# Pacing a kernel's gathers by TensorE's progress and feeding its pair products from SBUF alone

## The reference

```python
def _L0_rec_ref(inputs, W0, W1):            # inputs (b, 32 fields, 32 dims)
    x = inputs
    res = []
    for W in (W0, W1):
        prev = x.shape[1]
        z = jnp.einsum('bhd,bmd->bhmd', inputs, x).reshape(b, n * prev, k)
        x = jnp.einsum('bpd,pj->bjd', z, W)
        res.append(x)
    return jnp.sum(jnp.concatenate(res, axis=1), axis=-1)
...
e = jnp.stack([tbl_0[ids[:, 0]], ..., tbl_31[ids[:, 31]]], axis=1)
z = _L0_rec_ref(e, L0_rec_W0, L0_rec_W1)
h = jnp.concatenate([z, dense_ctx], axis=1)
h = jnp.maximum(h @ W_top1 + b_top1, 0.0)
h = jnp.maximum(h @ W_top2 + b_top2, 0.0)
y = h @ W_top3
```

## Time and profile before

| | before |
|---|---|
| median of 3 runs | 377.18 us (376.98 to 377.78) |
| span of the profiled execution | 597.7 us |
| own time of the profiled execution | none given beside the span |
| mean granted TensorE clock, profiled | 0.80 |
| PE busy, profiled | 412.6 us |
| DVE busy | 203.4 us |
| ACT busy | 235.5 us |
| POOL busy | 246.5 us |

### The profile page before, as it was taken

How to read it: one execution, slowest core, us unless ns; L and a number is a source line. 1 busy time by engine, 2 the same in 40 slices (tenths; PEclk the granted TensorE clock), 3 DMA queues, 4 the chain that set the end, 5 groups by cost and what they waited for, 6 DMA issues and landing times.

```text
span 597.7 us, 9512 instructions
## 1 busy us (share of the span) xinstructions
PE 412.6 (69%) x3656; PEld 360.8 (60%) x3656; DVE 203.4 (34%) x834; ACT 235.5 (39%) x774; POOL 246.5 (41%) x262
## 2 busy tenths in 40 slices
PE   5512112874257887877788778687787679999988
PEld 4301001653256776766666667577676668989988
DVE  4200000694723333322333233333332235556510
ACT  3300000662175334522343334433452237676641
POOL 6777772547055444544445554544444440000000
PEclk9755555795589877877787888977787779999999
DMA  8100000000000000000000000000000000000000
GB/s 299 45 14 13 13 13 6 11 3 14 2 10 10 8 10 7 10 8 9 9 9 10 10 10 9 11 8 9 8 10 8 8 10 2 2 2 2 2 2 1
DMA packets 10765, 9.66 MB, mean 16 GB/s; under 512 B 4664, under 2 KB 8896, under 8 KB 10720
## 3 DMA queue, kind: packets, MB, share of 16 engines
q0 software_dynamic: 8192, 4.21, 4.8%
q1 hardware_dynamic: 2528, 4.84, 2.3%
HBM read 9.03 MB, written 0.00 MB: 15 GB/s over the span
## 4 chain that ended last, share of the span: by engine, by line
PE 57%; issue 18%; another core or an unknown queue 11%; DVE 7%; ACT 6%; DMA 1%; SPq 0%; ACTq 0%
PE WA L725 20%; PE QB L697 10%; PE PA L687 8%; PE T L710 4%; DVE RT L421 4%; PE M L738 4%; PE M L757 2%; PE ET L674 2%; ACT eblk L285 2%; ACT TS L285 1%; PE PA L639 1%; PE M L764 1%; PE M L748 1%; ACT RT L285 1%
## 5 line engine op out<-in xcount | busy, mean ns | idle before, releaser
L278 POOL DMA_INDIRECT emb<-in_table,rows x256 | 245.8, 960 | 239.0 <-PE ET L674 165.3
L725 PE MATMUL WA<-TS,RX 128*128 128x128 f32 x896 | 127.0, 301 | 1.0 <-ACT TS L285 1.0
L584 DVE COPY TS<-T 32x64 f32<-32x64 f32 x256 | 55.5, 217 | 200.6 <-PE T L710 184.6
L725 PEld LDWEIGHTS WA<-TS,RX 128*128 128x128 f32 x896 | 119.7, 215 | 6.0 <-issue 6.0
L697 PE MATMUL QB<-eblk,zQ 128*64 128x68 f32 x1024 | 69.1, 243 | 74.3 <-issue 74.0
L697 PEld LDWEIGHTS QB<-eblk,zQ 128*64 128x64 f32 x1024 | 49.9, 146 | 89.8 <-issue 85.8
L552 DVE TENSOR_TENSOR zQ<-ET,eT 128x1024 f32<-128x1024 f32 x32 | 39.2, 1225 | 159.0 <-ACT eT L285 158.9
L687 PE MATMUL PA<-eblk,zP 128*128 128x132 f32 x512 | 80.6, 296 | 5.3 <-issue 3.4
L639 PE MATMUL PA<-sym,TS 128*128 128x272 f32 x64 | 29.4, 552 | 74.5 <-issue 47.3
L687 PEld LDWEIGHTS PA<-eblk,zP 128*128 128x128 f32 x512 | 73.4, 212 | 6.3 <-issue 4.9
L285 ACT ACTIVATE eblk<-ET 32x256 f32<-32x256 f32 x128 | 48.6, 380 | 71.0 <-PE ET L674 66.0
(11 more groups left out here) (87 smaller groups left out, 294.1 us busy)
## 6 DMA issues: line engine op xcount, KB each, us to landing
emb<-in_table,rows POOLq DMA_INDIRECT x256
TS<-in_W SPq DMA_DIRECT2D x8, 256.0 KB, 4.3
wt<-in_W_top SPq DMA_DIRECT2D x2, 512.0 KB
y1w<-in_W_rows SPq DMA_DIRECT2D x1, 448.0 KB
TS<-in_W_rows SPq DMA_DIRECT2D x1, 448.0 KB
sym<-in_W_cols SPq DMA_DIRECT2D x1, 264.0 KB, 2.8
TS<-in_W_cols SPq DMA_DIRECT2D x1, 264.0 KB, 3.1
idc<-in_ids SPq DMA_DIRECT2D x1, 128.0 KB, 2.0
```

What stands on the lines that cost most here:

```text
L278: eng.indirect_dma_start(emb[par][:, g, :], None, table, bass.IndirectOffsetOnAxis(rows[:, k, g:g + 1], 0))\
L584: eng.tensor_copy(view(ts[32 * q:32 * q + 32, :, :], P * REST + b0, [[4 * P, 2], [P, 4], [1, 8]]), view(src, q, [[C17, 2], [4, 4], [C33, 8 ...
L725: m = eng.matmul(WA[:, 0:P], C[:, kt, :], TS[k % 2][:, slot_of(kt), :], start=(kt == 0), stop=(kt == KT - 1))
```

## The change

- Gathers 16 to 27 wait for PE's step of W0 x W1 number 2(n - 16) + 9. From gather 28 on, every second gather waits for a step of PE: two gathers for each of the three trios of a unit and two for its last products (`t3_made`), 3.5 units ahead of the unit whose rows they fetch.
- `eT` gets 12 places for each group of eight fields: the eight and the first four again (TURN). ACT fills it with two copies, both ahead of the four into `eblk`, counted by `et_copied`.
- All products read `eT`, none reads ET. The products within a group become cyclic: distances 1 to 3 are one instruction with eight pairs each (768 elements per partition), the four pairs of distance 4 and half of the squares are another (256 elements). The columns' order changes with `off`. NZ goes from 11 to 5.
- The transposes of unit u + 1 stand behind the second trio of unit u (ET_STEP = 1), not ahead of its first. They wait for the copies out of ET only (`et_copied`, `eblk_made`), not for the products. ACT's copies for unit u + 1 move in the same way behind the copy of the second trio. ACT now waits for the products of the unit in front before it writes `eT`, and PE's first trio waits for `eblk_made` as well.

```diff
--- before.py
+++ after.py
@@ -19,6 +19,9 @@
 MORE = 16
 RTC = 2 * P + MORE
 RAB = HALF * HALF
+TURN = SUB + SUB // 2
+FREE = 16
+PACED = 28
 ONES = 16
 SLOTS = 59
 Y1T = 7
@@ -26,7 +29,7 @@
 
 def off(s):
 
-    return sum(SUB - r for r in range(1, s))
+    return SUB * (s - 1) if s <= SUB // 2 else SUB * (SUB - 1 - s) + s
 
 
 def pair_columns():
@@ -73,7 +76,7 @@
     C17 = HALF + 1
     EB = NQ * 2 * C17
     N1, N2 = H1 // P, H2 // P
-    NZ = 11
+    NZ = 5
     W1P = 8
     KT = 56
 
@@ -106,7 +109,7 @@
         wt3 = sb("wt3", [P, N2, P])
 
         emb = [sb(f"emb{i}", [P, P // NQ, D]) for i in range(2)]
-        eT = sb("eT", [P, GROUPS * F])
+        eT = sb("eT", [P, GROUPS * NQ, TURN])
         eblk = [sb(f"eblk{i}", [P, GROUPS, NQ, 2 * C17]) for i in range(2)]
         zP = [sb(f"zP{i}", [P, GROUPS, P]) for i in range(2)]
         zQ = [sb(f"zQ{i}", [P, GROUPS, 2, 64]) for i in range(2)]
@@ -163,6 +166,7 @@
         c_made = sem("c_made")
         c_kept = sem("c_kept")
         et_made = sem("et_made")
+        et_copied = sem("et_copied")
         eblk_made = sem("eblk_made")
         z_made = sem("z_made")
         p_made = sem("p_made")
@@ -236,6 +240,7 @@
 
 
         EARLY_AT = (8, 18)
+        ET_STEP = 1
 
         block = ctx.enter_context(nc.Block())
 
@@ -269,12 +274,24 @@
             eng.wait_ge(const_s, 1)
             eng.affine_select(out=ident[:, :], in_=ident[:, :], compare_op=ALU.not_equal, fill=1.0,
                               base=0, pattern=[[-1, P]], channel_multiplier=1).then_inc(const_s, 1)
+            def gate(n):
+
+                if FREE <= n < PACED:
+                    eng.wait_ge(rt_made, 2 * (n - FREE) + SUB + 1)
+                elif n >= PACED and n % 2 == 0:
+                    u, j = divmod(n - PACED, UG)
+                    if j // 2 < TRIOS:
+                        eng.wait_ge(p_made, TRIOS * u + j // 2 + 1)
+                    else:
+                        eng.wait_ge(t3_made, u + 1)
+
             eng.wait_ge(rows_made, 1)
             for k in range(TILES):
                 par = k % 2
                 for unit in range(UNITS):
                     wait(eng, et_made, UNITS * (k - 2) + unit + 1)
                     for g in range(UG * unit, UG * unit + UG):
+                        gate(UG * UNITS * k + g)
                         eng.indirect_dma_start(emb[par][:, g, :], None, table,
                                                bass.IndirectOffsetOnAxis(rows[:, k, g:g + 1], 0))\
                            .then_inc(gathered[par][unit], 16)
@@ -294,17 +311,19 @@
 
             def eblk_copy(u):
 
+                eng.wait_ge(et_made, u + 1)
+                wait(eng, z_made, NZ * u)
+                parts = ET[:, 0:GROUPS * F].rearrange("p (g i) -> p g i", i=SUB)
+                copy(eT[:, :, 0:SUB], parts).then_inc(et_copied, 1)
+                copy(eT[:, :, SUB:], parts[:, :, 0:TURN - SUB]).then_inc(et_copied, 1)
                 if u == 0:
                     eng.wait_ge(zeroed, 5)
                     eng.wait_ge(ones_set, 4 * NQ)
-                eng.wait_ge(et_made, u + 1)
                 wait(eng, t3_made, u - 1)
                 for v in range(NQ):
                     r = slice(DIM * v, DIM * v + DIM)
                     dst = view(eblk[u % 2][r, :, :, :], 2 * C17 * v + 1, [[EB, GROUPS], [C17, 2], [1, HALF]])
                     copy(dst, ET[r, 0:GROUPS * F].rearrange("p (g x h) -> p g x h", x=2, h=HALF)).then_inc(eblk_made, 1)
-                copy(eT[:, :], ET[:, 0:GROUPS * F]).then_inc(eblk_made, 1)
-
             def part_copy(t):
                 k, j = divmod(t, SLOTS_TILE)
                 unit, r = divmod(j, TRIOS)
@@ -382,9 +401,9 @@
             copy(wt3[:, :, 0], vec[:, N1 + N2:]).then_inc(wt3_made, 1)
             for t in range(TOTAL):
                 u, r = divmod(t, TRIOS)
-                if r == 0 and len(EARLY_AT) <= u + 1 < ALL:
+                part_copy(t)
+                if r == ET_STEP and len(EARLY_AT) <= u + 1 < ALL:
                     eblk_copy(u + 1)
-                part_copy(t)
                 if r == 0 and u > 0:
                     across_copy(u - 1)
                 if r < 2 and u > 0:
@@ -530,41 +549,33 @@
                     apart_across(1, 1, 0, HALF, True, added)
                     cross_second(1, 0, HALF, added)
 
-            def field(a, dims):
-                return view(ET[:, :], a, dims)
-
             def copied(a, dims):
-                return view(eT[:, :], a, dims)
+                return view(eT[:, :, :], a, dims)
 
             def products(u, part):
 
                 parts, sides = 4 * GROUPS, 2 * GROUPS
                 within, across, rest = zP[u % 2][:, :, :], zQ[u % 2][:, :, :, :], z3[u % 2][:, :, :]
 
-                def apart(s):
-                    some = [[SUB, parts], [1, SUB - s]]
-                    eng.tensor_tensor(view(within, off(s), [[32, parts], [1, SUB - s]]), field(0, some), copied(s, some),
-                                      ALU.mult).then_inc(z_made, 1)
-
                 if part == 0:
-                    eng.wait_ge(eblk_made, (NQ + 1) * (u + 1))
+                    eng.wait_ge(et_copied, 2 * (u + 1))
                     wait(eng, t3_made, u - 1)
                     eng.tensor_tensor(view(across, 0, [[64, sides], [SUB, SUB], [1, SUB]]),
-                                      field(0, [[HALF, sides], [1, SUB], [0, SUB]]),
-                                      copied(SUB, [[HALF, sides], [0, SUB], [1, SUB]]), ALU.mult).then_inc(z_made, 1)
+                                      copied(0, [[2 * TURN, sides], [1, SUB], [0, SUB]]),
+                                      copied(TURN, [[2 * TURN, sides], [0, SUB], [1, SUB]]), ALU.mult).then_inc(z_made, 1)
                 if part == 1:
-                    for s in range(1, 5):
-                        apart(s)
+                    turns = SUB // 2 - 1
+                    eng.tensor_tensor(view(within, 0, [[32, parts], [SUB, turns], [1, SUB]]),
+                                      copied(0, [[TURN, parts], [0, turns], [1, SUB]]),
+                                      copied(1, [[TURN, parts], [1, turns], [1, SUB]]), ALU.mult).then_inc(z_made, 1)
                 if part == 2:
-                    for s in range(5, SUB):
-                        apart(s)
-                    some = [[SUB, parts], [1, 4]]
-                    eng.tensor_tensor(view(within, PAIRS, [[32, parts], [1, 4]]), field(0, some), copied(0, some),
-                                      ALU.mult).then_inc(z_made, 1)
-                    some = [[F, GROUPS], [SUB, 4], [1, 4]]
-                    eng.tensor_tensor(view(rest, 0, [[THIRD, GROUPS], [4, 4], [1, 4]]), field(4, some), copied(4, some),
-                                      ALU.mult).then_inc(z_made, 1)
-                    eng.tensor_copy(view(rest, MORE, [[THIRD, GROUPS], [1, HALF]]), field(0, [[F, GROUPS], [1, HALF]]))\
+                    eng.tensor_tensor(view(within, off(4), [[32, parts], [4, 2], [1, 4]]),
+                                      copied(0, [[TURN, parts], [0, 2], [1, 4]]),
+                                      copied(4, [[TURN, parts], [-4, 2], [1, 4]]), ALU.mult).then_inc(z_made, 1)
+                    eng.tensor_tensor(view(rest, 0, [[THIRD, GROUPS], [4, 4], [1, 4]]),
+                                      copied(4, [[NQ * TURN, GROUPS], [TURN, 4], [1, 4]]),
+                                      copied(4, [[NQ * TURN, GROUPS], [TURN, 4], [1, 4]]), ALU.mult).then_inc(z_made, 1)
+                    eng.tensor_copy(view(rest, MORE, [[THIRD, GROUPS], [SUB, 2], [1, SUB]]), copied(0, [[NQ * TURN, GROUPS], [TURN, 2], [1, SUB]]))\
                        .then_inc(z_made, 1)
 
             def rest_copies(u, part):
@@ -668,7 +679,8 @@
             def emb_transposes(u):
                 k, unit = divmod(u, UNITS)
                 eng.wait_ge(gathered[k % 2][unit], 16 * UG * (k // 2 + 1))
-                wait(eng, z_made, NZ * u)
+                wait(eng, et_copied, 2 * u)
+                wait(eng, eblk_made, NQ * u)
                 for q in range(2):
                     g = UG * unit + NQ * q
                     t = eng.transpose(ET[:, P * q:P * q + P], emb[k % 2][:, g:g + NQ, :].rearrange("p g d -> p (g d)"), ident[:, :])
@@ -679,6 +691,7 @@
                 u, r = divmod(t, TRIOS)
                 if r == 0:
                     eng.wait_ge(z_made, NZ * (u + 1))
+                    eng.wait_ge(eblk_made, NQ * (u + 1))
                 if t == 0:
                     eng.wait_ge(rt_kept, F)
                     eng.wait_ge(rx_kept, F // 2)
@@ -799,9 +812,9 @@
                     emb_transposes(EARLY_AT.index(h))
             for t in range(TOTAL):
                 u, r = divmod(t, TRIOS)
-                if r == 0 and len(EARLY_AT) <= u + 1 < ALL:
+                triples(t)
+                if r == ET_STEP and len(EARLY_AT) <= u + 1 < ALL:
                     emb_transposes(u + 1)
-                triples(t)
                 if r == TRIOS - 1:
```

## The result

The changed kernel takes 401.77 us (median of five runs, 397.35 to 402.67) against 377.18 (376.60 to 377.78): a ratio of 1.063 [1.059, 1.067]. The forecast was slower, by 11.5 us; it is slower by 24.6. The time lies in the range of 369 to 412.

The account below looks back on a forecast made before the run. POOL's chain of gathers was taken as the bound, 369.7 us before. After: 338.2 (last gather landed) + 38.0 (remainder) + 4.9 (hold) = 381.1, 11.5 more; 377.18 + 11.5 = 388.7 us, range 369 to 412.

Parts of the forecast that it names:

- Which chain ends last: PE's chain put at 366.2 us, POOL's chain of gathers at 369.7 before the change; POOL's the longer.
- The prediction's own test: If removing the gate alone doesn't win back some 6 us, the gathers' chain is not what sets the end.
- the gate's term: Gather 60 waits for tile 1's first trio and starts at 88.7 us instead of 79.2; POOL never catches up.
- the hold's term: Gathers meeting SBUF-only products on DVE take longer: 0.2 us per unit, 4.9 us over 24.5 units.
- last gather to the end: Behind unit 31's transposes, now 2.9 us later in unit 30, 38.0 us remain instead of 40.95.
- around the span: The 7.5 us from POOL's chain of 369.7 us to the median of 377.18, taken as lying around the span.
- the landing: A gather takes 5.8 us from start to landed, read from the first unit's last gather.
- long lock: Rival: runs of SBUF-pair work on DVE hold gathers long; 413 us at 1.2 us per unit, 445 at 2.5; chance 0.16.
- The transposes' place: Behind the second trio, 4.4 us from transposes to products is hidden under 5.4 us of PE work; costed at nothing.
- The products: Eleven DVE instructions become five, the cyclic ones 0.95 and 0.43 us; 2.85 instead of 3.2 us per unit.
- POOL quick: Rival: gathers closer than 1.25 us apart in the runs; below 1.19, 374.7 us, faster by 0.65%; chance 0.22.
- dripping: Rival: PE's single matmuls with issue gaps are partly in the runs and pacing ends them; down to 364 us; chance 0.11.

Follow-up runs that it names:

- SBUF-only products: Kernel before with both operands of every product read from eT in SBUF, old places and eleven instructions, no gate: 420.97 us, ratio 1.114.
- no adds: Kernel before with tile 0's 128 symmetrising adds each replaced by a memset of the same destination: 368.14 us, ratio 0.976.
- second profile: Kernel before, no edit, profiled once more: 379.58 us in the one run, span 377.8 us.
- gate alone: Kernel before with only the waits on gathers added: 380.35 us, ratio 1.0082.
- PSUM products and no gate: Changed kernel with one operand of every product from ET in PSUM and without the waits on gathers: 377.53 us, ratio 0.998.
- The transposes in front again: Changed kernel with the transposes and ACT's copies of them ahead of the first trio again: 404.51 and 408.75 us.

## Why the prediction was right in kind and wrong in size

*Which chain ends last: right.* POOL's gathers set the end in both kernels; PE waits for the last ones in both profiles. Two edits of DVE's instructions show it besides: SBUF-only products (+43 us) and no adds (-9.4 us). Gather 255 starts at 376.92, 334.48 and 322.48 in SBUF-only products, the kernel before and no adds, and each time 43.3 to 43.4 us follow it to the end of the span. The prediction's own test failed all the same: taking the gate away was to win back some 6 us, and it didn't. The test rested on the gate's price, not on the chain, as the table shows.

What the sum put at what, and what the profiled executions of both kernels show (us):

| | put at | measured |
|---|---|---|
| gather 60 starts later (the gate's term) | 9.5 | 2.4, all of it holds |
| gather 60 to 255 (the hold's term) | 4.9 | 18.0 |
| last gather to the end | -2.9 | -2.7 |
| sum | 11.5 | 17.7 |

The timed medians are 24.6 apart. The other 6.9 are scatter between executions: that of the kernel before was profiled 2.4 us above its median and that of the changed kernel 4.4 below. What differs between them isn't shown.

*The gathers' hold by SBUF-only products: the mechanism right, the term mis-sized, and this is the step that failed.* It was put at 0.2 us per unit, 4.9 in all. From gather 60 to 255 the changed kernel took 261.5 us against 243.5 in the kernel before: 18.0 us, or 0.74 per unit. With the 2.4 us up to gather 60 the hold grew by 20.4 us. Undoing that part alone gives 22.3 us back in the timed runs. The value was chosen near the median of eight meetings, most of them with short adds. The right row was there: the add of 1.09 us had held its gather to its own end, and the sum should have taken "to the end of the instruction" as the rule. For a 1.22 us product and gathers at random that gives an estimate of 0.6 us (in 1.22 of 1.25 cases, half of 1.22 on average). The remainder comes from the phase: zQ starts some 3.4 us behind the start of a unit's last gather (203.53 and 206.96 in the unit shown, by way of landing, transposes and copy), and the third start behind that one, at 3.74 us, falls early into zQ. In the sixteen units from 185 us on it is always this gather that meets zQ, 0.06 to 0.41 us into zQ, and it is held up by 0.83 us on average. In the units before, other gathers meet zQ, mostly later in it.

*What tile 0's adds do to gathers before: left out of the sum.* They were weighed only as evidence on a lock. In fact they delay gather 60 by 12.0 us before any change (91.01 in the second profile; without the adds 79.05). The 7.5 us "around the span" were mostly that: the span lies only 1.8 us under the time in both kernels' profiles. A second error hid part of it: the landing was put at 5.8 us, from the first unit, and in the second profile unit 31's transposes run 2.3 us behind the start of the last gather. The long lock was called unlikely because only 7.5 us were left for it; this was the place where it hid.

*The gate: the second step that failed.* Gather 60 was to come 9.5 us later by waiting for PE. In the changed kernel it came 2.4 us later, and POOL waited at no gate: up to gather 60 the holds are 14.4 us instead of 12.0, and they are the whole difference. POOL's lead had already gone. With the gate alone it came 0.4 us later; timed, that costs 3.1 us. So in the profiled executions this term was 9.5 us too large and the hold 15.5 too small. That the one made up for most of the other in the sum is luck.

*The transposes' place: right.* 38.3 us remain behind them, for 38.0, and the products stay covered. The edit by itself wins more than its 2.9 us, because it also changes what the gathers meet. A wait was missed: ACT's second `rest_copies` now stand behind its ET copies, and PE's `other_triples` waits for them, 11.1 us in 21 waits. With gathers as the bound it costs nothing.

*The products: right.* 0.95 and 0.42 us for the two cyclic ones (0.95 and 0.43 predicted), zQ 1.22 from SBUF as from PSUM. By an estimate from the TRN2 errata table of the Trainium skill ("VectorE: DVE Perf Modes") each product would be 65 ns shorter from SBUF. That doesn't show: zQ took 1,225 ns on average before and 1,224 after. (The 1.40 us of the prediction is the seven zP alone; with the eighth removed instruction it is 1.60, and the saving of 0.35 us is right.)

*The rivals.* POOL's spacing in the profiles without the stalls is the same 1.25 us, so "POOL quick" falls. The dripping of the earlier trace rows wasn't in the runs in a form that pacing could end: the gate alone made the kernel slower. "Long lock" was the nearer of the rivals in mechanism: dense runs do hold a gather for 3 us and more, but the products of the changed kernel release it at the end of zQ, in all 26 cases from gather 60 on. The Trainium skill ("SBUF — State Buffer", two separate sides) has such a lock as exclusive and for the whole instruction. These rows agree as to the hold on the gather, 0.36 to 1.03 us until zQ's end. They also show that the hold can last over many instructions. The other half of what the Trainium skill says there, that whichever starts first blocks the other, they don't show: where zQ began beside a gather already under way, the gather took its 0.94 or 0.95 us and zQ its 1.20 to 1.23. That the cause is a lock and not something else the two share is the Trainium skill's reading; the runs show the hold and what brings it about.

The version with PSUM products and no gate stays at 377.5 because another chain has come up: PE and ACT by turns, 37.3 us a tile, where the prediction had 36.3 for PE. Which copy or wait in it would have to go stays open; moving ACT's copies to DVE didn't shorten it. No version that keeps tile 0's adds beats the kernel before by more than its measurement is uncertain.

## What to carry to other kernels

Before moving a VectorE operand from PSUM to SBUF, look at what GpSimd does meanwhile: if it issues indirect gathers back to back and they set the end, every SBUF-pair instruction can cost up to its own length, and several back to back can cost more than the longest of them. To price it, ask at which moment of the instruction the gather starts, not what a typical meeting cost. Pacing a producer that is slower than its consumer won nothing here; each wait it meets is lost unless something else had already taken its lead. Time left over between a sum and a measurement is a term not yet found, and not an argument against one.

## What the runs showed of the hardware that wasn't expected

A gather of 0.94 us took up to 11.9 us of POOL in tile 0, beside runs of short adds with both operands in SBUF (4.60 us in the rows shown), and beside memsets or products with one operand in PSUM 0.94 to 0.96. Beside a product of 1.22 us with both operands in SBUF it went on at that product's end if DVE had been waiting ahead of it, and 1.7 us later than alone, behind four such products, if DVE had come straight from another instruction (five of six meetings from gather 60 on, in The transposes in front again). The same code was profiled twice at 597.7 and at 377.8 us. The first had PE issuing single matmuls about a microsecond apart while gathers ran; the second didn't, and the timed runs agree with the second.
